# The narrow score tile as one plain fp32 product, five slots for value tiles, and a new order of the streams

## The chip, the cores and the metric

The kernel runs on one core of one Trainium2 chip. The metric is the device time of one execution in microseconds (us); the spans and instruction times below come from one profiled execution. Engines are named as in the profile: PE (TensorE matmul), PEld (its weight loads), ACT (ScalarE), DVE (VectorE), POOL (GpSimd), SP (SyncE, which issues all DMAs here).

## The reference, cut to what matters

Two sequences of 4096 rows with 256 channels pass through single-head causal attention with a residual and a layernorm, then through a router that sends the top 75% of the rows through one 256x256 block with a gelu, then through a residual and a layernorm again.

```python
qkv = x @ w_attn + b_attn
q, k, v = jnp.split(qkv, 3, axis=-1)
attn = jnp.einsum('btc,bsc->bts', q, k) / jnp.sqrt(Cv) + mask      # causal
attn = jax.nn.softmax(attn, axis=-1)
out = jnp.einsum('bts,bsc->btc', attn, v) @ w_proj + b_proj
x = layernorm(x + out)
scores = jnp.einsum('bld,d->bl', x, w_router)                      # top_k: 75% of the rows
processed = gelu(selected @ w_block)
x = layernorm(x + x.at[batch_idx, top_idx].set(processed))
```

All of it is fp32, and which rows are routed hangs on small differences, so the kernel keeps near-fp32 precision in its matmuls.

## The kernel before, in words

**Groups and tiles.** The rows of queries are cut into 16 groups of 512 (8 in each sequence; `G` counts them). The weights of queries and keys are multiplied into one matrix `A` ahead of time, so that the scores of a group are `xT` (the transposed input, the keys' side) against `qT`. A score tile holds 128 keys (partitions) by up to 512 queries (columns). Each group has four tiles on its diagonal, of 512, 384, 256 and 128 columns (tile `i` starts at column `128*i`, `start_col`), and one full tile for each 128 keys before it. The last of the four, 128x128, is the narrow tile of the group. In the last group the diagonal tiles stand at the end of the group, in all others at its start.

**Split products.** Operands of precise matmuls are kept as two fp32r parts, a high one and a low one, made by a rounding copy and a subtraction. `split3` (line 580 on; the matmul itself is line 587) issues three products for each chunk of 128 channels, high by high, high by low and low by high: six matmuls for one score tile.

**Stages of a group.** The projection of queries (`pe_q`) fills a bank of PSUM, ACT writes its high part with a bias (`qhi`, line 932), DVE the low part (`qlo`, line 937). Projected values get the same treatment and go to DRAM (`vstore`, line 985), from where SP loads one 128-row tile at a time into one of `NV` slots of `vs` (`load` in `values`, line 1184): 256 KB each. The load into a slot waits until PE has used its former tile. Scores go to one of two banks `sbank`, ACT copies each into the `ring` of 34 slots (line 1021), DVE adds the mask to diagonal blocks (line 1029) and keeps a running maximum. At the end of a group PE turns the maximum (lines 1111 and 1134), DVE subtracts it (line 1147), ACT takes the exponential (line 1154) and rounds a high part (line 1161), DVE makes the low part (line 1166), and PE multiplies by the values (lines 1230 to 1232 for the first three groups of each sequence, 1236 to 1238 for the others and 1200 to 1202 for the last four tiles). Projection, scores and values of neighbouring groups, and the block behind the router (line 1642 and `split3` into `fbank`), are interleaved on PE.

**What sets the order.** Every piece of work is given to `at(engine, stream, make)`. Within a stream the order is fixed; between the streams of an engine a planner (`planned`) chooses ahead of time, one operation after the other: it holds a table of costs for each engine, takes operations that could start, and prefers the one with the longest chain behind it plus the stream's preference (`PREFER_US`, and `BEFORE_LAST_US` and `LAST_US` in the last two groups); `MARGIN_US` lets a stream's operation be passed over until it has been ready for so long. The result is one fixed list of instructions on each engine, and waits on semaphores between them. The SP list is in order as well: a DMA that must wait holds up those behind it.

**The end.** After the last values PE turns the output back, DVE evaluates the residual and the statistics (`last chain`), a search of eight rounds between DVE and PE (lines 1788, 1844, 1799) finds the threshold of the router, and 16 predicated copies (line 2037) and stores finish. ACT copies the last sums (`ot`, line 1299) and normalizes rows (`norm`, line 1457) there.

Of the kernel before, what the change touches and what calls it, by code (L numbers as in the profile page):

```python
# [16 lines left out]
P = 128  # L17
# [13 lines left out]
NV = 6  # L31
# [28 lines left out]
PREFER_US = {"final result": 2182, "scores copy": 1183, "prepare keys": 1153, "final pick": 1052,  # L60
             "project vhi": 1018, "prepare late": 997, "attention_out aggr": 988, "attention_out norm": 969,
             "project vlo": 917, "prepare xlo": 911, "prepare bias": 864, "project qhi": 759, "project qlo": 745,
             "final load": 741, "attention_out ot": 637, "late load": 622, "final store": 544, "ffn scale": 520,
             "project xlo": 468, "final choose": 418, "search first": 405, "project load": 386, "ffn flo": 367,
             "attention_out store": 363, "ffn rows": 359, "bias columns": 313, "attention_out score": 280,
             "last chain": 188, "row_max": 177, "attention_out load": 128, "attention_out evac": 127,
             "ffn store": 113, "row_max reduce": 93, "softmax lo": 31, "softmax z": 27, "search": 23,
             "softmax hi": -20, "project xhi": -21, "final_roots own": -28, "scores running": -67,
             "attention_out stats": -77, "softmax exp": -128, "attention_out router": -177, "final_roots": -177,
             "ffn fhi": -248, "ffn stats": -290, "ffn gelu": -305, "scores hide": -360, "last": -381,  # L70
             "prepare": -424, "final sums": -456, "last router": -540, "project vstore": -783,
             "attention_out istd": -834, "late": -837, "values load": -896, "attention_out residual": -1389,
             "ffn aggr": -1397, "final own": -1468, "ffn add": -1565, "ffn sums": -1808, "final scale": -1950}
MARGIN_US = {"late": 8, "project xhi": 8, "prepare bias": 8, "final_roots": 8, "attention_out store": 8,
             "final scale": 5, "final sums": 5, "ffn add": 5, "final own": 3, "ffn scale": 3, "prepare keys": 3,
             "ffn rows": 3, "ffn sums": 3, "attention_out norm": 2, "ffn aggr": 2, "ffn stats": 2,
             "final_roots own": 2, "softmax exp": 1.5, "final result": 1.5, "last router": 1.5, "project vlo": 1.5,
             "row_max reduce": 1.5, "search": 1.5, "attention_out residual": 1.5, "project xlo": 1.5,
             "attention_out load": 1.5, "bias columns": 1.5, "late load": 1.5, "values load": 1.5,
             "attention_out score": 1, "attention_out stats": 1, "prepare late": 1, "scores hide": 1,  # L80
             "final load": 1, "project load": 1, "out": 0.6, "proj": 0.6, "attention_out ot": 0.6, "ffn gelu": 0.6,
             "attention_out aggr": 0.6, "ffn flo": 0.6, "final choose": 0.6, "prepare xlo": 0.6,
             "attention_out istd": 0.6, "ffn store": 0.6, "final store": 0.6, "project vstore": 0.6, "scores": 0.3,
             "values": 0.3, "project qhi": 0.3, "project vhi": 0.3, "attention_out evac": 0.3, "search first": 0.3}
BEFORE_LAST_US = {"project xlo": 1066, "attention_out ot": 1012, "final_roots own": 733, "ffn aggr": 721,
                  "project load": 677, "attention_out load": 630, "last router": 576, "prepare keys": 528,
                  "last chain": 492, "final choose": 481, "prepare late": 380, "softmax lo": 322,
                  "row_max reduce": 318, "attention_out residual": 315, "ffn stats": 307, "last": 278,
                  "final sums": 260, "proj": 230, "ffn rows": 224, "project vlo": 141, "project qlo": 134,
                  "search first": 96, "softmax hi": 52, "prepare xlo": 47, "scores copy": 42, "search": 40,  # L90
                  "bias columns": 39, "row_max": 4, "attention_out evac": -7, "attention_out norm": -11,
                  "values": -17, "scores running": -27, "final pick": -39, "ffn flo": -101,
                  "attention_out stats": -105, "attention_out istd": -147, "attention_out aggr": -150,
                  "scores hide": -176, "attention_out store": -188, "project qhi": -193, "out": -211,
                  "ffn gelu": -214, "project vhi": -228, "late": -229, "softmax exp": -229, "softmax z": -245,
                  "values load": -252, "ffn add": -278, "ffn fhi": -300, "ffn sums": -310, "project vstore": -311,
                  "prepare": -321, "late load": -322, "final own": -333, "ffn scale": -374, "prepare bias": -438,
                  "project xhi": -539, "ffn store": -554, "final scale": -560, "final load": -591,
                  "final result": -644, "final_roots": -733, "attention_out score": -873,
                  "attention_out router": -931, "final store": -1016}  # L100
LAST_US = {"last": 970, "final sums": 866, "values load": 854, "project vhi": 796, "ffn scale": 793,
           "final load": 773, "attention_out norm": 684, "attention_out evac": 659, "ffn sums": 657,
           "prepare bias": 651, "search": 552, "softmax hi": 545, "project qlo": 458, "ffn gelu": 411,
           "attention_out residual": 379, "project xlo": 339, "ffn store": 333, "scores hide": 305,
           "project load": 301, "ffn flo": 220, "ffn stats": 218, "ffn fhi": 199, "attention_out store": 146,
           "prepare late": 132, "attention_out ot": 95, "row_max": 90, "final scale": 88, "prepare xlo": 70,
           "softmax lo": 56, "scores running": 48, "attention_out aggr": 30, "scores": 14, "final pick": -5,
           "proj": -17, "late": -63, "attention_out istd": -65, "final_roots": -71, "project qhi": -93,
           "ffn aggr": -117, "search first": -123, "attention_out stats": -131, "last router": -131,
           "row_max reduce": -139, "scores copy": -141, "prepare": -154, "ffn rows": -191, "out": -206,  # L110
# [227 lines left out]
def program(nc, x, xt, w_attn_t, columns, w_proj, b_proj, w_router, w_block, out):  # L338
# [65 lines left out]
    with ctx:  # L404
# [25 lines left out]
        with nc.sbuf_tensor("xraw", [P, CC, GQ], F32) as xraw_:  # L430
            xraw = xraw_
# [1614 lines left out]
        for G in range(len(groups)):  # L2046
            ordered[:] = [G]
            if G:
                project_load(G)
# [127 lines left out]
```

## Time and profile before

| | us |
|---|---|
| median of 3 runs | 954.7 (954.55, 954.7, 959.75) |
| span of the profiled execution | 953.7 |
| PE busy | 931.6 (98%) |
| DVE busy | 785.4 (82%) |
| ACT busy | 633.7 (66%) |
| POOL busy | 305.0 (32%) |
| DMA, mean over 16 engines | 51.0% of the span, 155.84 MB |
| mean granted TensorE clock | 0.992 |

The profiled execution gives its span, 953.7 us from the first instruction to the last; no time of its own outside the span is listed for it, and the median of the runs lies 1.0 us above the span. A PE interval is busy from a matmul's start to its modelled end, so neighbouring matmuls overlap, and the time that a group of them takes is read from its start to the start of what follows.

### The profile page before, as it was taken

Reading aid. Unit: us, or ns where it says so; the run is one execution under the profiler, and the core shown is the slowest. Engines: PE = TensorE matmul, PEld = TensorE weight load, DVE = VectorE, ACT = ScalarE, POOL = GpSimd, SP = SyncE. Lnnn points to the kernel's source line nnn. Section 1 sums busy time; section 2 is a strip of 40 time slices with the busy share of each in tenths; the row PEclk is TensorE's granted clock in tenths of the full one; section 3 lists DMA queues with packets and bytes.
Section 4 is the critical chain, followed back from the end, with each engine's and each line's share of the span. In section 5 each row is a group of like instructions: output and inputs, shape, how many; then the busy total and the mean of one; then the engine's idle time right before and its main releaser. Section 6 shows DMA issues by size and latency. Waiting matters only on the chain.

```text
span 953.7 us, 15684 instructions
## 1 busy us (share of the span) xinstructions
PE 931.6 (98%) x5030; PEld 798.6 (84%) x5030; DVE 785.4 (82%) x1497; ACT 633.7 (66%) x1011; POOL 305.0 (32%) x460
## 2 busy tenths in 40 slices
PE   9999999999999999999999999999999999999992
PEld 6889998888888888888888999888888888888871
DVE  5898887866994896589879999998699799659977
ACT  3576665864774594479565866677578569547994
POOL 3541141242230335333325361452022244301243
PEclk9999999999999999999999999999999999999996
DMA  6644344344353355468634534346777734437934
GB/s 193 206 123 154 104 144 122 103 144 152 101 185 113 111 155 175 146 205 263 195 104 149 189 93 142 130 123 207 234 238 226 242 113 134 150 105 238 323 124 177
DMA packets 89044, 155.84 MB, mean 163 GB/s; under 512 B 8442, under 2 KB 18300, under 8 KB 88964
## 3 DMA queue, kind: packets, MB, share of 16 engines
q1 hardware_dynamic: 88964, 154.85, 51.0%
q8 instruction: 41, 0.67, 0.3%
q14 instruction: 39, 0.32, 0.1%
HBM read 114.96 MB, written 39.86 MB: 162 GB/s over the span
## 4 chain that ended last, share of the span: by engine, by line
PE 85%; DVE 7%; ACT 4%; issue 2%; DMA 1%; DVEq 0%; SPq 0%; ACTq 0%
PE sbank L587 37%; PE fbank L587 12%; PE obank L1236 9%; PE obank L1237 9%; PE obank L1238 9%; PE obank L1232 2%; PE obank L1230 2%; PE obank L1231 2%; DVE ring L1147 1%; ACT parts L1161 1%; DVE ring_lo L1166 1%; ACT ring L1154 1%; DMA ring<-xt 1%; DVE tail L2037 1%; PE mbank L1134 1%
## 5 line engine op out<-in xcount | busy, mean ns | idle before, releaser
L587 PE MATMUL sbank<-qT,xT 128*128 128x512 f32 (+2 forms) x1728 | 406.6, 377 | 1.1 <-ACT ring L1021 1.0
L587 PEld LDWEIGHTS sbank<-qT,xT 128*128 128x128 f32 x1728 | 306.4, 188 | 54.9 <-ACT ring L1021 1.1
L1021 ACT COPY ring<-sbank 128x512 f32<-128x512 f32 (+3 forms) x286 | 157.2, 553 | 178.3 <-PE sbank L587 125.1
L1166 DVE TENSOR_TENSOR ring_lo<-ring,parts 128x1024 fp32r<-128x1024 f32 (+4 forms) x174 | 181.1, 1050 | 32.2 <-ACT parts L1161 31.4
L1161 ACT CAST parts<-ring 128x1024 fp32r<-128x1024 f32 (+4 forms) x174 | 145.0, 843 | 48.1 <-PE obank L1238 34.1
L1070 DVE TENSOR_TENSOR runmax<-ring,runmax 128x1024 f32<-128x1024 f32 x84 | 107.1, 1274 | 69.0 <-ACT ring L1021 68.1
L1147 DVE TENSOR_TENSOR ring<-ring,mbank 128x1024 f32<-128x1024 f32 (+4 forms) x174 | 157.0, 955 | 5.6 <-PE mbank L1134 5.3
L1236 PE MATMUL obank<-ring_lo,vs 128*128 128x512 f32 (+3 forms) x416 | 158.9, 382 | 0.2 <-DVE ring_lo L1166 0.2
L1238 PE MATMUL obank<-parts,vs 128*128 128x512 f32 (+3 forms) x416 | 157.4, 378 | 0.0
L1237 PE MATMUL obank<-parts,vs 128*128 128x512 f32 (+3 forms) x416 | 157.4, 378 | 0.0
L1154 ACT ACTIVATE ring<-ring 128x1024 f32<-128x1024 f32 (+4 forms) x174 | 142.2, 852 | 9.7 <-DVE ring L1147 9.5
L1238 PEld LDWEIGHTS obank<-parts,vs 128*128 128x128 f32 x416 | 78.2, 188 | 14.6
L1236 PEld LDWEIGHTS obank<-ring_lo,vs 128*128 128x128 f32 x416 | 78.3, 188 | 14.3 <-issue 0.9
L1237 PEld LDWEIGHTS obank<-parts,vs 128*128 128x128 f32 x416 | 78.3, 188 | 13.3
L1674 POOL TENSOR_TENSOR yb<-xres,yb 128x512 f32<-128x512 f32 x28 | 39.1, 1418 | 140.2 <-ACT yb L1595 76.5
L1291 POOL TENSOR_TENSOR xres<-xres,b_tot 128x512 f32<-128x512 f32 x30 | 44.5, 1505 | 55.5 <-DMA xres<-x 53.1
L894 POOL TENSOR_TENSOR xT<-xraw,xT 128x512 fp32r<-128x512 f32 x27 | 37.9, 1422 | 64.4 <-ACT xT L876 63.4
L1570 POOL TENSOR_TENSOR ot_sb<-ot_sb,yb 128x512 f32<-128x512 f32 x16 | 22.6, 1413 | 102.5 <-PE fbank L1328 80.1
L587 PE MATMUL fbank<-WV,xT 128*128 128x256 f32 x384 | 51.5, 284 | 0.0
L1065 DVE TENSOR_TENSOR runmax<-ring,runmax 128x512 f32<-128x512 f32 (+3 forms) x73 | 43.3, 594 | 9.7 <-ACT ring L1021 7.6
L587 PEld LDWEIGHTS fbank<-WV,xT 128*128 128x128 f32 x384 | 49.6, 191 | 1.7
L587 PE MATMUL fbank<-xT,A 128*128 128x512 f32 x180 | 46.1, 392 | 0.2 <-DVE qT L937 0.2
(268 smaller groups left out, 1371.4 us busy)
## 6 DMA issues: line engine op xcount, KB each, us to landing
vs<-v_scratch SPq DMA_DIRECT2D x288, 256.0 KB, 2.9
v_scratch<-vnew SPq DMA_DIRECT2D x30, 512.0 KB, 3.5
out<-tail SPq DMA_DIRECT2D x32, 256.0 KB, 2.6
xres<-x SPq DMA_DIRECT2D x15, 512.0 KB, 3.9
x_scratch<-xres SPq DMA_DIRECT2D x14, 512.0 KB, 3.9
y_scratch<-yb SPq DMA_DIRECT2D x14, 512.0 KB, 3.0
tail<-x_scratch SPq DMA_DIRECT2D x28, 256.0 KB, 3.6
tail<-y_scratch SPq DMA_DIRECT2D x28, 256.0 KB, 4.3
```

The source lines that it names most:

```text
L587: mm = eng.matmul(o, lhs(lh, k), rhs(rh, k), start=n == 0, stop=n == len(todo) - 1)
L1021: act.copy(slot(n)[:, c0:], sbank[n % NSS][:, c0:]).then_inc(a_copy, 1)
L1065: dve.tensor_tensor(runmax[:, 0, c0:], slot(n)[:, c0:], runmax[:, 0, c0:], ALU.max).then_inc(v_max, 1)
L1070: dve.tensor_tensor(runmax[:, :, :], slots(ns, 0), runmax[:, :, :], ALU.max).then_inc(v_max, 1)
L1147: dve.tensor_tensor(slots(ns, c0), slots(ns, c0), mbank[:, None, c0:].broadcast_to([P, len(ns), GQ - c0]), ALU.subtract).then_inc(v_z, 1)
L1154: act.activation(slots(ns, c0), slots(ns, c0), ACT.Exp, scale=SCALE).then_inc(a_exp, 1)
L1161: act.copy(hi_of(u), slots(ns, c0)).then_inc(a_hi, 1)
L1166: dve.tensor_tensor(slots_lo(ns, c0), slots(ns, c0), f32(hi_of(u)), ALU.subtract).then_inc(v_lo, 1)
L1236: pe.matmul(o, vh, lo_, start=n == first_tile[G], stop=False)
L1237: pe.matmul(o, vh, hi_, start=False, stop=False)
L1238: mm = pe.matmul(o, vl, hi_, start=False, stop=last)
L1291: pool.tensor_tensor(r[:, 2 * j:2 * j + 2], r[:, 2 * j:2 * j + 2], b_tot[:, None, :].broadcast_to([P, 2, C]), ALU.add).then_inc(g_xres, 1)
```

## The change

The narrow tile is no longer a split product. Two buffers are added, `x_narrow` and `q_narrow`, each 128 partitions by 2 chunks by 128 columns of plain fp32. SP loads `x_narrow` from the transposed input (one DMA for each group, 128 KB), and ACT writes `q_narrow` from the same PSUM bank as `qhi`, with the bias, without rounding to fp32r (two more activations for each group). PE then issues two fp32 matmuls where six fp32r matmuls stood. The low part `qlo` now waits for `q_narrow` as well, ACT waits with `q_narrow` until the narrow tile of the group before has been multiplied, and PE waits with the narrow tile for the load and for `q_narrow`. `NV` falls from 6 to 5. All four preference tables are replaced, which moves instructions on every engine.

```diff
-NV = 6
+NV = 5
...
-PREFER_US = {"final result": 2182, "scores copy": 1183, "prepare keys": 1153, "final pick": 1052,
+PREFER_US = {"final choose": 6932, "prepare keys": 5298, "ffn store": 4854, "scores copy": 4501, "bias columns": 3716,
...
+    narrow_no = {G: n for n, (G, _, i) in enumerate(tiles) if i == QT - 1}
...
+        x_narrow = sb("x_narrow", [P, CC, P])
+        q_narrow = sb("q_narrow", [P, CC, P])
...
+        def narrow_load(G):
+
+            b, g = groups[G]
+
+            def load(sp):
+                if G:
+                    sp.wait_ge(p_s, narrow_no[G - 1] + 1)
+                else:
+                    sp.wait_ge(ld_wv, 16)
+                sp.dma_start(x_narrow[:, :, :], xt_rows[b][:, :, (g + 1) * GQ - P:(g + 1) * GQ]).then_inc(ld_xn, 16)
+            at("sp", "project narrow", load)
...
             act.activation(qT[:, G % 2, 0, m], bank_of(("q", G, m))[:, :], ACT.Identity,
                            bias=ucol[:, m:m + 1]).then_inc(a_qhi, 1)
+                if G:
+                    act.wait_ge(p_s, narrow_no[G - 1] + 1)
+                act.activation(q_narrow[:, m], bank_of(("q", G, m))[:, GQ - P:GQ], ACT.Identity,
+                               bias=ucol[:, m:m + 1]).then_inc(a_qn, 1)
 
             def qlo(dve, m):
                 dve.wait_ge(a_qhi, CC * G + m + 1)
+                dve.wait_ge(a_qn, CC * G + m + 1)
...
-                split3(pe, sbank[n % NSS][:, c0:], lambda h, k: xT[:, h, k, kt * P:(kt + 1) * P],
-                       lambda h, k: qT[:, G % 2, h, k, c0:], CC).then_inc(p_s, 1)
+                if n == narrow_no[G]:
+                    pe.wait_ge(ld_xn, 16 * (G + 1))
+                    pe.wait_ge(a_qn, CC * (G + 1))
+                    for k in range(CC):
+                        mm = pe.matmul(sbank[n % NSS][:, c0:], x_narrow[:, k, :], q_narrow[:, k, :], start=k == 0,
+                                       stop=k == CC - 1)
+                    mm.then_inc(p_s, 1)
+                else:
+                    split3(pe, sbank[n % NSS][:, c0:], lambda h, k: xT[:, h, k, kt * P:(kt + 1) * P],
+                           lambda h, k: qT[:, G % 2, h, k, c0:], CC).then_inc(p_s, 1)
```

**Order on ACT at the start.** Before, `qT` is the high part of the first queries, the copies from `sbank` are those of the first group's four score tiles, and `xT<-ring` is the high part of the next group's input (`xhi`):

```order
L932 ACTIVATE qT<-fbank,ucol 128x512 x2
L876 CAST xT<-ring 128x2x512
L1021 COPY ring<-sbank 128x512
L1021 COPY ring<-sbank 128x384
L876 CAST xT<-ring 128x2x512
L1021 COPY ring<-sbank 128x256
L1021 COPY ring<-sbank 128x128
```

and in the changed kernel (its line numbers are 5 to 33 higher):

```order
L950 ACTIVATE qT<-fbank,ucol 128x512
L954 ACTIVATE q_narrow<-fbank,ucol 128x128
L950 ACTIVATE qT<-fbank,ucol 128x512
L954 ACTIVATE q_narrow<-fbank,ucol 128x128
L1052 COPY ring<-sbank 128x512
L1052 COPY ring<-sbank 128x384
L1052 COPY ring<-sbank 128x256
L894 CAST xT<-ring 128x2x512
```

The two `q_narrow` stand between and behind the two `qT`; the first three score copies now stand ahead of the cast of the next input.

**Order on ACT at the end of the last group**, from the rounding of the 384-column tile (`parts<-ring 128x384`) to that of the last two tiles; `ot_sb` is the copy of the sums, `tail<-xres` the normalization of group 14, `tail<-tail,fin` a final scaling. Before:

```order
L1161 CAST parts<-ring 128x384
L2022 ACTIVATE tail<-tail,fin 128x256 x2
L2027 ACTIVATE tail<-tail,fin 128x256
L1457 ACTIVATE tail<-xres,rstd,rs_h 128x256 x4
L1299 COPY ot_sb<-sbank 128x512 x2
L1161 CAST parts<-xraw 128x256
L1161 CAST parts<-xraw 128x128
```

and now:

```order
L1488 ACTIVATE tail<-xres,rstd,rs_h 128x256
L1192 CAST parts<-ring 128x384
L2058 ACTIVATE tail<-tail,fin 128x256 x3
L2053 ACTIVATE tail<-tail,fin 128x256
L1330 COPY ot_sb<-sbank 128x512 x2
L1192 CAST parts<-xraw 128x256
L2053 ACTIVATE tail<-tail,fin 128x256
L2058 ACTIVATE tail<-tail,fin 128x256
L1192 CAST parts<-xraw 128x128
```

The four normalizations have moved ahead of the rounding of the 384-column tile, so four scalings alone stand directly before the copy of the sums.

**Order on SP at the start**, from the router's weights on. `xres` is the residual input of groups 0 and 1 (512 KB each), `ring<-xt` the transposed input of groups 1 and 2 (512 KB each). Before:

```order
L678 DMA wr<-w_router 128x256
L856 DMA ring<-xt 128x2x512 x2
L1282 DMA xres<-x 128x4x256 x2
L856 DMA xraw<-xt 128x2x512
```

and now:

```order
L683 DMA wr<-w_router 128x256
L1313 DMA xres<-x 128x4x256 x2
L874 DMA x_narrow<-xt 128x2x128
L862 DMA ring<-xt 128x2x512 x2
L862 DMA xraw<-xt 128x2x512
```

The transposed input of the next groups is now issued behind 1 MB of residual input and the new 128 KB.

## Rows read from the trace of the kernel before

**Rows 1.** The page: span, and busy us of each engine (share) and instructions.
```profile
span 953.7 us, 15684 instructions
PE 931.6 (98%) x5030; PEld 798.6 (84%) x5030; DVE 785.4 (82%) x1497; ACT 633.7 (66%) x1011; POOL 305.0 (32%) x460
```

**Rows 2.** Busy time by stretch: start, middle, end; from:to, length, engines, PEclk, DMA, GB/s.
```profile
0.00:30.00 30.00, 27.69 (x147) 21.83 (x148) 15.31 (x42) 11.19 (x17) 13.05 (x40) 1.00 0.62 195
30.00:912.50 882.50, 881.63 (x4746) 761.30 (x4745) 737.23 (x1341) 594.88 (x936) 275.08 (x378) 1.00 0.52 164
912.50:953.70 41.20, 22.24 (x142) 15.44 (x140) 32.85 (x115) 27.65 (x61) 16.86 (x43) 0.81 0.33 122
```

**Rows 3.** Timeline of PE around a narrow tile; start us, us, instruction.
```profile
118.51 0.78 PE L587 MATMUL sbank<-qT,xT 128*128 128x128 f32 x6
119.13 0.33 PE L1230 MATMUL obank<-vs,ring_lo 128*128 128x256 f32 x1
```

**Rows 4.** Groups of PE by line and shape: the narrow tile's matmuls.
```profile
L587 PE MATMUL sbank<-qT,xT 128*128 128x128 f32 x96 | 12.8, 269 | 0.0
```

**Rows 5.** Timeline of PE: plain fp32 matmuls of 256 columns and of one.
```profile
931.88 1.03 PE L1642 MATMUL obank<-runmax,late_x 128*128 128x256 f32 x4
932.75 0.27 PE L1844 MATMUL fbank<-cmp,ones_bf 128*128 128x120 bf16 x2
...
14.10 0.50 PE L704 MATMUL mbank<-bcols,ring 128*128 128x1 f32 x4
14.46 1.31 PE L587 MATMUL sbank<-qT,xT 128*128 128x384 f32 x6
```

**Rows 6.** Groups of ACT by line and shape.
```profile
L1021 ACT COPY ring<-sbank 128x512 f32<-128x512 f32 x240 | 140.2, 587 | 157.4 <-PE sbank L587 106.4 <-PE obank L1238 50.5
L932 ACT ACTIVATE qT<-fbank,ucol 128x512 fp32r<-128x512 f32 x32 | 22.0, 690 | 22.6 <-PE fbank L587 19.4 <-PE fbank L922 3.2
L1021 ACT COPY ring<-sbank 128x128 f32<-128x128 f32 x15 | 3.9, 263 | 3.8 <-PE sbank L587 3.8
```

**Rows 7.** Timeline of the start on PE, ACT and DVE.
```profile
10.41 1.27 ACT L932 ACTIVATE qT<-fbank,ucol 128x512 fp32r<-128x512 f32 x2 [3.23 <-PE fbank L922]
11.13 1.41 DVE L937 SCALAR_TENSOR_TENSOR qT<-fbank,ucol,qT 128x512 fp32r<-128x512 f32 x2 [1.97 <-ACT qT L932]
12.64 1.62 PE L587 MATMUL sbank<-qT,xT 128*128 128x512 f32 x6
15.98 1.04 ACT L876 CAST xT<-ring 128x1024 fp32r<-128x1024 f32 x1 [4.31 <-DMA ring<-xt]
17.57 0.98 PE L587 MATMUL sbank<-qT,xT 128*128 128x256 f32 x6 [1.00 <-ACT ring L1021]
```

**Rows 8.** Busy time by stretch: the last 28 full value tiles, and the DVE's fullest stretch; columns as in rows 2.
```profile
870.70:909.80 39.10, 39.10 (x177) 32.27 (x178) 38.04 (x71) 39.04 (x58) 5.99 (x10) 1.00 0.90 298
...
500.00:600.00 100.00, 100.00 (x648) 90.74 (x647) 94.01 (x225) 68.81 (x116) 43.82 (x65) 1.00 0.44 139
```

**Rows 9.** Value loads: whole program, 870:875, 905:909 (KB each, median us to landing), then their extremes.
```profile
vs<-v_scratch SPq DMA_DIRECT2D x288, 256.0 KB, 2.9
...
vs<-v_scratch SPq DMA_DIRECT2D x2, 256.0 KB, 2.8
...
vs<-v_scratch SPq DMA_DIRECT2D x2, 256.0 KB, 5.6
...
DMA to landing us min/median/max: 2.5/2.9/6.0
```

**Rows 10.** Timeline of SP in the last group: two final loads between value loads.
```profile
900.59 2.91 SPq L1184 DMA_DIRECT2D vs<-v_scratch  x3
903.66 0.32 SPq L1970 DMA_DIRECT2D tail<-x_scratch  x1
904.03 0.42 SPq L1971 DMA_DIRECT2D tail<-y_scratch  x1
904.55 3.02 SPq L1184 DMA_DIRECT2D vs<-v_scratch  x3
```

**Rows 11.** Timeline of the end on PE, ACT and DVE.
```profile
909.55 0.39 PE L1238 MATMUL sbank<-parts,vs 128*128 128x512 f32 x1
...
909.98 2.06 ACT L1457 ACTIVATE tail<-xres,rstd,rs_h 128x256 f32<-128x256 f32 x4
911.95 1.04 ACT L1299 COPY ot_sb<-sbank 128x512 f32<-128x512 f32 x2
...
912.54 0.90 DVE L1312 TENSOR_TENSOR ot_sb<-obank,ot_sb 128x256 f32<-128x256 f32 x2 [2.25 <-ACT ot_sb L1299]
...
912.71 0.28 PE L1202 MATMUL obank<-parts,vs 128*128 128x256 f32 x1
913.11 0.83 PE L1328 MATMUL fbank<-ident,ot_sb 128*128 128x128 f32 x4
...
940.16 9.85 DVE L2037 COPY_PREDICATED tail<-mbank,tail 128x512 f32<-128x512 uint32 x16
```

More of the change, by code:

```diff
@@ L58 @@
 TABLE_US = 1.28
-PREFER_US = {"final result": 2182, "scores copy": 1183, "prepare keys": 1153, "final pick": 1052,
[L61 to L110, printed above, removed]
-           "final store": -206, "project vlo": -231, "final result": -232, "final own": -247, "final choose": -268,
-           "project vstore": -269, "project xhi": -283, "ffn add": -287, "softmax exp": -289, "last chain": -306,
-           "bias columns": -324, "prepare keys": -359, "softmax z": -360, "values": -380, "final_roots own": -398,
-           "attention_out score": -424, "late load": -541, "attention_out router": -610, "attention_out load": -649}
@@ new lines @@
+MARGIN_US = {"late": 14.3, "project load": 11.6, "project vstore": 8, "last": 7, "final choose": 5, "final pick": 5,
+             "final scale": 5, "project xhi": 5, "search first": 5, "bias columns": 4.8, "ffn rows": 4.6,
+             "project narrow": 4, "ffn scale": 3, "final sums": 3, "attention_out istd": 2.6,
+             "attention_out norm": 2.2, "ffn stats": 2.2, "row_max reduce": 2, "final own": 1.8, "final load": 1.7,
+             "ffn flo": 1.5, "ffn gelu": 1.5, "late load": 1.5, "prepare bias": 1.5, "prepare xlo": 1.5,
+             "final result": 1.3, "softmax exp": 1.2, "final_roots": 1.1, "attention_out load": 1, "last router": 1,
+             "project vlo": 1, "project xlo": 1, "attention_out evac": 0.6, "attention_out stats": 0.6,
+             "ffn aggr": 0.6, "final store": 0.6, "out": 0.6, "scores": 0.6, "scores hide": 0.6, "values": 0.6,
+             "attention_out store": 0.5, "values load": 0.5, "attention_out ot": 0.3, "ffn sums": 0.3, "proj": 0.3,
+             "project vhi": 0.3, "search": 0.3, "softmax hi": 0.3, "project qhi": 0.1}
@@ L494, in program @@
         mt_ps = mbank[:, :].rearrange("p (t k) -> p t k", t=QT)
+        ld_xn, a_qn = sem("ld_xn"), sem("a_qn")
         ld_qk, ld_b, ld_w, ld_ffw, ld_xt = sem("ld_qk"), sem("ld_b"), sem("ld_w"), sem("ld_ffw"), sem("ld_xt")
@@ L831, in bias_load @@
                     sp.dma_start(b_cols[:, k:k + 1], b_dram[k * P:(k + 1) * P].rearrange("(p a) -> p a", a=1)).then_inc(ld_bc, 16)
+            narrow_load(0)
             at("sp", "bias columns", bias_store)
@@ L2049, in program @@
                 project_load(G)
+            if G:
+                narrow_load(G)
             project(G)
```

45 lines of the change are left out of this document (added).

## The prediction

> **What bounds the kernel now.** I read the page's busy line first: PE is busy for 98% of a span of 953.7 us, DVE for 82%, ACT for 66% [rows 1]. A mean hides stages, so the busy time by stretch comes next [rows 2]. From 30 us to 912.5 us PE is busy for 881.63 of 882.50 us. In the first 30 us it idles 2.3 us, and in the last 41.2 us it works for little more than half: there DVE and ACT carry the chain. So 92% of the span is the sum of PE's matmuls; what counts there is PE work removed, and any new wait is added in full. The granted clock is 1.00 (2.4 GHz) in the first two stretches, 0.81 on the mean in the end, and nothing in the change gives PE a reason to slow down earlier. The timeline of PE gives prices of work from start to start, which the overlapping durations do not.
>
> **The change part by part**, against the profiled span of 953.7 us; the median of the runs is 1.0 us more.
>
> *The narrow tile on PE.* Six fp32r matmuls start at 118.51 and what follows at 119.13 [rows 3]: 0.62 us, 0.103 us each; there are 96 of them, so 16 tiles [rows 4]. Two plain fp32 matmuls come instead. The trace records a plain fp32 matmul as two weight loads with two matmuls. With 256 columns four such records (two products) take 0.87 us, from 931.88 to 932.75; with one column four take 0.36 us, from 14.10 to 14.46 [rows 5]. 128 columns lie between. The 256-column price is nearer to a price per column, so half of it, 0.43 us, still above the 0.36 us that a record costs without columns; I take 0.43. Gain: 16 x (0.62 - 0.43) = **3.0 us**, all on PE's filled stretch. Bounds: 16 x (0.62 - 0.36) = 4.2 us gained, and 16 x (0.87 - 0.62) = 4.0 us lost.
>
> *`q_narrow` on ACT.* A 128-column copy takes 0.26 us; the bias costs 0.690 - 0.587 = 0.10 us more [rows 6], so 0.37 us, 32 times: 11.8 us of ACT, which has 320 us free [rows 1]. In groups 1 to 15 the queries are projected ahead and other work of PE covers the 0.37 us by which `qlo` is later; without that cover it would be 15 x 0.7 = 10 us at worst. In group 0 nothing covers it: the two `qhi` start at 10.41, `qlo` at 11.13, PE's first scores at 12.64 [rows 7]. With a `q_narrow` behind each `qhi` the second `qlo` starts some 0.7 us later, less the time it stood behind the first: **+0.6 us**.
>
> *The order of the start.* PE waited 1.00 us at 17.57 for a score copy, because ACT stood at the cast of the next input until its DMA landed at 15.98 [rows 7]. Now three copies stand ahead of that cast: -1.0 us. Against it the same input is issued behind 1.1 MB more; at the 195 GB/s of this stretch [rows 2] that is some 5 us, of which PE has two fills of values (24 matmuls) and the narrow tile to work on. I set these against each other, for **-1.0 us** in all, bounds -2 and +3 (the 5 us less some 2 us of moved work).
>
> *The slots of values.* In the last group PE takes 28 tiles in 39.1 us, 1.40 us each [rows 8]. With six slots a load has five tiles, 7.0 us, from its slot being free to its use; with five it has 5.6 us. Loads land after 2.8 us at the beginning of this stretch and 5.6 us at its end; 6.0 us is the longest of the program [rows 9]. Each third one is issued 0.89 us late behind two final loads (903.66 to 904.55) [rows 10]. So in the last third, with the DMA engines at 0.90, a load can be late by 0.9 us; with fewer loads under way each should land a little sooner. A late load stops PE, and the four tiles after it are then early. I take **+0.8 us**; nothing at the low end, and at the high end 28/5 x 0.9 = 5 us. Before that, scores stand between the value tiles, a load has over 10 us, and the cover is wide. Queued behind a held value load are final loads alone.
>
> *The 16 loads of `x_narrow`*: 2 MB on 156 MB, 16 places in SP's list, each held until the narrow tile of the group before is through PE. That tile is at the head of its group and the next one a whole group later (in the last group at its end), so the load has at least 10 us where a value load takes 2.9. **0**, bounds 0 and +1: what is queued behind a held one is a value load, and these have the slack above.
>
> *The end.* PE finished the sums at 909.94. ACT copied them at 911.95 only, since four normalizations stood ahead; DVE waited 2.25 us, and PE could turn the output at 913.11 instead of 912.83 when its own work was through [rows 11]. Now the normalizations come earlier and scalings that need no new data take their place. The copy may be 1 us sooner, of which the first turn takes 0.3 and the second half, whose rounding on ACT and low part on DVE stand behind the same copy, more: **-0.6 us**, bounds -1.5 and +1. The search and the 16 predicated copies (9.85 us) stay as they are.
>
> *The order of the middle.* It has 0.87 us of PE idle to give [rows 2], and small gaps under the modelled ends. What it can lose is open. DVE is at 94% between 500 and 600 us [rows 8], with ACT's new work ahead of it. I take 0, bounds -2 and +5.
>
> Sum: 953.7 - 3.0 + 0.6 - 1.0 + 0.8 - 0.6 = 950.5 us; with the 1.0 us of the runs **951.5 us**.
>
> **The rivals.**
>
> *A: the fifth slot and the new order are paid for by PE (slower).* Place: the last 28 value tiles, and DVE's full stretch. It decides once loads land later than 5.6 us after their slot is free. At 0.9 us in each five tiles that is 5 us instead of 0.8; a further 3 us of waits in the middle gives 951.5 + 4.2 + 3 = 958.7, and the first part alone 955.7. For it: landing times grow to 5.6 us just there. Against it: the median is 2.9 us.
>
> *B: fp32 costs by count of passes (slower).* If a plain product went through PE as four passes at the floor of 0.103 us that the six pay now, the tile would take 8 x 0.103 = 0.83 us: 16 x 0.21 = 3.3 us lost instead of 3.0 gained, 951.5 + 6.3 = 957.8. The trace speaks against the floor being paid four times: it shows two records for each product and 0.09 us for one. The Trainium skill (FP8 and Floating Point Precision, section TensorE Precision Notes) says that true fp32 takes four passes through the array, and so stands against replacing three reduced products by one exact one; by its count the change has eight passes where six were. In streaming time the trace agrees with it: 0.87 us for two products of 256 columns is four clocks of 2.4 GHz for each column.
>
> *C: the new order gives more than I see.* Several small gaps of the middle and of the end go: narrow tile 4.2, start 2, end 1.5, no slot loss, 2 in the middle, about 9 us at most; half of the surplus over my sum gives 947 to 948. Against more: PE's work itself is untouched.
>
> *D: the narrow tile saves nothing* (the new waits on PE, for the load and `q_narrow`, eat it): 951.5 + 3.0 = 954.5.
>
> **How the numbers follow.** My forecast (949 to 953.5) 0.42; D and its neighbourhood (to 955) 0.15; A 0.20, of it 0.04 beyond 1%; B 0.06; C 0.17, of it 0.03 beyond 1%. The range leaves out the outer half of C's reach and the outer parts of A: **946.5 to 958**. A measurement of this kernel tells 1%, 9.5 us, from no change. Faster by more than that (under 945.2) needs all low bounds at once: 0.03. Slower (over 964.2) needs the open loss of the middle beyond its bound: 0.05. Within: 0.92.
>
> **What would show it.** Right: 64 records for the narrow tile, 0.43 us from its start to what follows; PE idle under 2 us between 30 us and the end of the values, and that end near 908 to 909; no PE idle with a value load as releaser; DVE's wait at the sums near 1 us. Wrong: narrow tiles of 0.6 us or more (B, D); PE or its weight loads released by `vs` from 890 us on (A); PE stretches with idle behind DVE in the middle.

## The result: 8 us slower, and the trace after

The changed kernel takes 963.8 us (median of five executions), the kernel before 955.7 us beside it: 1.0082 times the time, 95% interval 1.0064 to 1.0100. One of the five was in a slow state and took 2404.0 us; the ratio leaves it out. The prediction was 951.5 us with a range of 946.5 to 958. It is wrong in sign, and the time lies outside the range.

The profiled execution of the changed kernel has a span of 960.4 us (before 953.7). Its page, which answers to [rows 1]:

```profile
span 960.4 us, 15711 instructions
PE 928.8 (97%) x4998; PEld 793.9 (83%) x4998; DVE 792.4 (83%) x1497; ACT 637.9 (66%) x1041; POOL 310.3 (32%) x460
```

PE works 2.8 us less and idles 31.6 us where it idled 22.1. The windows say where; they are cut, like [rows 2], at 30 us and near the last matmul of the values that PE issues before it first turns the output:

```profile
0.00:30.00 30.00, 27.64 (x148) 21.44 (x149) 16.43 (x43) 12.43 (x22) 12.04 (x40) 1.00 0.65 211
30.00:918.85 888.85, 879.73 (x4712) 757.10 (x4711) 744.19 (x1343) 598.46 (x965) 281.46 (x379) 1.00 0.52 164
918.85:960.40 41.55, 21.42 (x142) 15.36 (x140) 31.74 (x112) 27.06 (x56) 16.82 (x43) 0.80 0.38 138
```

In the first 30 us PE idles as much as before. The middle, which had 0.87 us of PE idle, has 9.12. The cut at the end doesn't fall at quite the same instruction in the two kernels. By the start of the matmul itself (912.71 us before, 918.73 now) the end is 0.7 us longer, and 6.0 of the 6.7 us of span lie ahead of it. PE's granted clock is 1.00 in the first two stretches, as before, and 0.80 in the last (0.81).

The narrow tile on PE, for [rows 3] and [rows 4] (a piece of PE's timeline, then its group):

```profile
119.32 0.61 PE L1033 MATMUL sbank<-q_narrow,x_narrow 128*128 128x128 f32 x4
119.69 0.36 PE L1261 MATMUL obank<-vs,ring_lo 128*128 128x256 f32 x1
119.89 0.28 PE L1262 MATMUL obank<-vs,parts 128*128 128x256 f32 x1
...
L1033 PE MATMUL sbank<-q_narrow,x_narrow 128*128 128x128 f32 x64 | 9.7, 274 | 0.0
```

It is 0.37 us to the next start (before 0.62). But part of the tile is hidden in the spacing of what follows. To the second start behind it there are 0.57 us, and before 0.79:

```profile
118.51 0.78 PE L587 MATMUL sbank<-qT,xT 128*128 128x128 f32 x6
...
119.30 0.28 PE L1231 MATMUL obank<-vs,parts 128*128 128x256 f32 x1
```

So a tile saves 0.22 us and 16 save 3.5. What PE waited for (line and releaser: us, times, longest), the whole span, the longest first:

```profile
PE mbank L1165 <- DVE mcol L1159: 5.1, 5, 1.5
PE mbank L1142 <- DVE runmax L1096: 3.1, 4, 1.5
PE obank L1673 <- issue: 1.9, 1, 1.9
...
PE obank L1267 <- issue: 0.8, 1, 0.8
...
PE obank L1231 <- DMA vs<-v_scratch: 0.3, 1, 0.3
```

The two on top are new: in the kernel before these two waits were 0.2 us each.

```profile
PE mbank L1134 <- DVE mcol L1128: 0.2, 1, 0.2
PE mbank L1111 <- DVE runmax L1065: 0.2, 1, 0.2
```

`L1142` is PE's turning of the running maximum into `mbank` (once for a group, four transposes), `L1165` the turning back of the column of maxima `mcol` that DVE has made of it at `L1152` to `L1159`. PE issues in order. When it comes to one of them and DVE isn't there yet, all the matmuls behind it stand. The fifth slot shows in one wait of 0.3 us. The 0.8 us at `L1267` have no releaser in the view, but their place in time has one, DVE's `ring_lo`:

```profile
702.88 1.20 DVE L1197 TENSOR_TENSOR ring_lo<-ring,parts 128x1024 fp32r<-128x1024 f32 x1
704.18 0.47 PE L1267 MATMUL obank<-ring_lo,vs 128*128 128x512 f32 x1 [0.82 <-issue]
```

### The profile page after: what moved, and what is told of

The parts are those of the page before. It is cut to its first block, busy times and chain, and to the rows that moved or that the text cites. A ratio compares the mean times of both kernels' runs of the same rounds, so it can differ in the third digit from the quotient of the medians.

```text
span 960.4 us, 15711 instructions
## 1 busy us (share of the span) xinstructions
PE 928.8 (97%) x4998; PEld 793.9 (83%) x4998; DVE 792.4 (83%) x1497; ACT 637.9 (66%) x1041; POOL 310.3 (32%) x460
## 4 chain that ended last, share of the span: by engine, by line
PE 79%; DVE 12%; issue 4%; POOL 3%; ACT 1%; DMA 1%; SPq 0%; DVEq 0%; ACTq 0%; POOLq 0%
PE sbank L592 33%; PE fbank L592 11%; PE obank L1269 8%; PE obank L1268 8%; PE obank L1267 8%; DVE ring_lo L1197 2%; DVE ring L1178 2%; PE obank L1261 2%; PE obank L1263 2%; PE obank L1262 2%; DVE runmax L1101 1%; PE mbank L1165 1%; DVE tail L2068 1%; DVE bnst L1385 1%; DVE runmax L1096 1%
## 5 line engine op out<-in xcount | busy, mean ns | idle before, releaser
L592 PE MATMUL sbank<-qT,xT 128*128 128x512 f32 (+2 forms) x1632 | 398.9, 384 | 0.6 <-issue 0.6
L592 PEld LDWEIGHTS sbank<-qT,xT 128*128 128x128 f32 x1632 | 294.4, 188 | 53.4 <-issue 1.0
L1197 DVE TENSOR_TENSOR ring_lo<-ring,parts 128x1024 fp32r<-128x1024 f32 (+4 forms) x174 | 176.7, 1023 | 23.6 <-ACT parts L1192 23.3
L1267 PE MATMUL obank<-ring_lo,vs 128*128 128x512 f32 (+3 forms) x416 | 158.4, 381 | 0.8 <-issue 0.8
L1101 DVE TENSOR_TENSOR runmax<-ring,runmax 128x1024 f32<-128x1024 f32 x84 | 109.3, 1301 | 53.5 <-ACT ring L1052 52.6
L1267 PEld LDWEIGHTS obank<-ring_lo,vs 128*128 128x128 f32 x416 | 78.3, 188 | 15.2 <-issue 1.5
```

Of the source, the lines that this page charges most:

```text
L592: mm = eng.matmul(o, lhs(lh, k), rhs(rh, k), start=n == 0, stop=n == len(todo) - 1)
L1101: dve.tensor_tensor(runmax[:, :, :], slots(ns, 0), runmax[:, :, :], ALU.max).then_inc(v_max, 1)
L1197: dve.tensor_tensor(slots_lo(ns, c0), slots(ns, c0), f32(hi_of(u)), ALU.subtract).then_inc(v_lo, 1)
L1267: pe.matmul(o, vh, lo_, start=n == first_tile[G], stop=False)
```

## Why DVE is late: two kinds of lateness

The longest waits lie at groups 0, 2, 6, 7, 11 and 13. Group 2, on DVE, GpSimd and PE, in the changed kernel:

```profile
75.25 0.69 DVE L1152 TENSOR_REDUCE mcol<-mbank 128x4 f32<-128x512 f32 x1
75.97 0.86 DVE L1157 TENSOR_TENSOR mcol<-mcol,row_const 128x4 f32<-128x4 f32 x1
76.87 1.19 DVE L1159 TENSOR_TENSOR mcol<-mcol,row_const 128x4 f32<-128x4 f32 x1
...
75.51 2.53 POOL L912 TENSOR_TENSOR xT<-xraw,xT 128x512 fp32r<-128x512 f32 x2 [6.47 <-ACT xT L894]
...
78.11 0.65 PE L1165 MATMUL mbank<-ident,mcol 128*128 128x128 f32 x4 [1.35 <-DVE mcol L1159]
```

The same step in the kernel before, with GpSimd idle from 72 to 80 us:

```profile
76.16 0.69 DVE L1121 TENSOR_REDUCE mcol<-mbank 128x4 f32<-128x512 f32 x1
76.88 0.16 DVE L1126 TENSOR_TENSOR mcol<-mcol,row_const 128x4 f32<-128x4 f32 x1
77.08 0.16 DVE L1128 TENSOR_TENSOR mcol<-mcol,row_const 128x4 f32<-128x4 f32 x1
```

Two additions on four numbers per partition, 0.16 us each, take 0.86 and 1.19 us. They end within 0.02 us of the one and the other of GpSimd's two subtractions, which take some 1.3 us each. The reduction ahead of them, which reads PSUM, keeps its 0.69 us. The same happens at groups 0 (0.85 and 1.20 us) and 7 (0.75 and 1.19). So these additions of DVE, with both operands in SBUF, stand still while GpSimd runs its subtraction. The Trainium skill (SBUF — State Buffer, section SBUF: two separate sides) states it: DVE and GpSimd share a pair of ports under an exclusive lock, and a DVE operation with two SBUF inputs waits for the whole of a GpSimd instruction that holds it. The trace agrees with it: both additions end with GpSimd's operations.

The kernel before has such meetings too: one addition takes 1.19 us at group 5, and one 0.53 us at groups 7 and 11. They cost PE 0.2 us in all. At groups 7 and 11 its turning stands 1.1 us and more behind the end of the additions in any case, and at group 5 it waits 0.18 us. What the new order changed is where the meetings fall, and how near PE's row stands behind them.

The second kind is the row. Group 6, DVE and then PE:

```profile
324.64 0.69 DVE L1609 TENSOR_TENSOR x1p<-ot_sb,vnew_b 128x512 fp32r<-128x512 f32 x1 [2.48 <-ACT vnew_b L1605]
326.10 0.29 DVE L1060 TENSOR_TENSOR ring<-ring,mask 128x128 f32<-128x128 f32 x1 [0.77 <-ACT ring L1052]
326.31 0.68 DVE L1152 TENSOR_REDUCE mcol<-mbank 128x4 f32<-128x512 f32 x1
...
327.44 0.65 PE L1165 MATMUL mbank<-ident,mcol 128*128 128x128 f32 x4 [1.55 <-DVE mcol L1159]
```

DVE idles 2.48 us at the head of its row for `x1p`, which waits for ACT and, behind it, GpSimd. It then waits 0.77 us more for the copy that it adds the mask to. The reduction behind both could have started at 323.5. Before, the same two stood ahead of it, but the operand of `x1p` was there at 323.08:

```profile
323.08 1.29 DVE L1578 TENSOR_TENSOR x1p<-ot_sb,vnew_b 128x512 fp32r<-128x512 f32 x2
324.49 0.69 DVE L1121 TENSOR_REDUCE mcol<-mbank 128x4 f32<-128x512 f32 x1
```

## Experiments

The planner sets every row from tables, so any edit moves rows everywhere. To change one thing alone, the runs below take the order of each engine from a list that is written out (`ORDERS`, the rows of one of the two kernels, engine by engine):

```diff
-    orders, times = planned(todo, signalled, urgency(todo), favours)
+    orders, times = pinned(todo)
```

Each time is the median beside runs of the kernel before on the same chip, and the ratio, with its 95% interval, is to those; their median lay between 954.9 and 955.2 us. By the traces e1, e4 and e7 have the changed kernel's sequence of work on PE, ACT, DVE and GpSimd, and e3, e8 and e12 that of the kernel before. **Theory O**: the new order costs it, where PE stands in front of a maximum that DVE has not made. Rivals: **Q** (`q_narrow`'s reads and waits), **S** (the fifth slot), later **P** (GpSimd over DVE), **E** and **W** (a gap closed opens elsewhere).

### Is it the order or the work?

**e1**, the old work in the new order: `before`, ORDERS = rows of the changed kernel without its 16 narrow loads.

> The work of the kernel before (narrow tile as six fp32r products, no q_narrow, no x_narrow, six value slots), but every engine issues its rows in the order of the changed kernel, written out, without the 16 narrow loads. Theory O (the order that the new preferences give makes PE stand in front of turned maxima and maxima columns that DVE has not made yet): the order's cost stays and the narrow tile's saving is gone, so about 4 us above the changed kernel, 966 to 969, with PE idle near 32 us. Rival Q (q_narrow's 32 reads on ACT, and DVE's qlo behind them, cost it): 954 to 957. Rival S (the fifth value slot costs it): 954 to 957, since there are six slots here.

Measured: 962.9 us, ratio 1.0085 (1.0071 to 1.0099). Its waits of PE:

```profile
PE mbank L1200 <- DVE mcol L1194: 4.8, 5, 1.4
PE mbank L1177 <- DVE runmax L1131: 2.8, 3, 1.5
```

The order alone costs 8 us, with none of the new work in the kernel. By the trace nearly all of it lies in the middle: the last matmul of the values starts at 920.52 us, 7.8 us later than before, of 7.9 us of span (961.6). Q and S fall as causes of the order's cost. The figure of 966 to 969 was too high: I had added the whole narrow saving to the changed kernel's time.

**e2**, the new work in the old order: the changed kernel, ORDERS = rows of `before`.

> The work of the changed kernel (fp32 narrow tile from x_narrow and q_narrow, five value slots), but PE, ACT, DVE and POOL issue in the order of the kernel before, written out; the three last tiles of group 8 stand a few rows earlier on PE and ACT, since q_narrow of group 9 waits for them, and SP's loads are moved by up to five rows, with the 16 narrow loads among them. Theory O: the narrow tile's saving of 16 x 0.25 us is left, 955.7 - 4 = 951 to 952.5. Rival Q or S: the cost of 8 us or more comes with the work, 959 to 964.

Measured: 956.3 us, 1.0006 (0.9992 to 1.0021). This is neither case: the 8 us are gone, but the saving isn't there either. One part was my own doing: where the tiles of group 8 had been moved, PE waited 1.3 us at 464.8 for DVE's `row_const`.

**e3**, five slots alone: `before` with

```diff
-NV = 6
+NV = 5
```

> The kernel before with five value slots in place of six and nothing else of the change; its order is written out, SP's loads moved by up to five rows so that none waits for a slot ahead of a store that it holds up. Theory O: 955 to 956.5. Rival S: 960 or more, with PE waiting for vs<-v_scratch in more than one place.

Measured: 955.9 us, 1.0005 (0.9992 to 1.0018); PE waits for a value load once, 0.8 us. S falls: the slot costs about half a microsecond in this order (-0.8 to +1.7 by the interval).

**e4**, `q_narrow` once:

```diff
-                if G:
-                    act.wait_ge(p_s, narrow_no[G - 1] + 1)
-                act.activation(q_narrow[:, m], ...)
+                if G == 0:
+                    act.activation(q_narrow[:, m], ...)
```

> The changed kernel in its own order, but q_narrow is written for group 0 alone and read by all 16 narrow tiles, so that 30 ACT reads of fbank and DVE's waits for them are left out (the narrow tiles of groups 1 to 15 are computed from group 0's queries). Theory O: within 1.5 us of the changed kernel, 962 to 964. Rival Q: back to 955 to 957.

Measured: 963.8 us, 1.0093 (1.0078 to 1.0109). Q falls in this order: DVE waited 11.9 us for `q_narrow` in the changed kernel, and without 30 of the 32 reads nothing is won: the waits at `mbank` are 8.0 us as before (8.2), and the one for `ring_lo` near 705 us has grown from 0.8 to 1.9 us, which may hide a gain of 1 us.

### What in the order?

**e5**, eleven rows moved, on DVE and PE:

```diff
 DVE  + row_max reduce 6   ahead of x1p          PE  + turning back, group 0: 1 row later
      + last maxima 10, 11, 13 ahead of softmax lo    + both turnings, group 2: 1 and 2 rows later
      + row_max reduce 13  ahead of router sums       + turning back, group 7: 2 rows later
```

> The changed kernel with all its work, its order written out and changed in eleven rows alone: on DVE the last steps of the running maximum of groups 10, 11 and 13 stand ahead of softmax lo and of a final result, and the reductions of groups 6 and 13 ahead of x1p and of four router sums; on PE the turning of groups 0, 2 and 7 stands one to three rows later. Theory O (order): the eight gaps of PE in front of mbank, 8.3 us in the trace, go all but a little, so 956 to 957.5. Rival E (the order's cost is spread, and a gap closed here opens elsewhere): 961 or more.

Measured: 960.1 us, 1.0056 (1.0042 to 1.0070). The waits at `mbank` fell from 8.2 to 1.3 us, the time by 3.7 us (medians), the span by 2.6. At 417.8 us PE now waited 1.5 us for `qT` behind a turning that had been moved, and at 420.4 us 1.0 us for `ot_sb`. So a part of the gaps closed came back elsewhere. The time lies between the two expectations.

**e7** moves no row. It lets GpSimd begin later:

```diff
                     pool.wait_ge(a_xhi, G + 1)
+                    if G in (2, 6, 12):
+                        pool.wait_ge(v_mc, 3 * {2: 1, 6: 3, 12: 8}[G])
```

> The changed kernel in its own order; only GpSimd's low halves of xT for groups 2, 6 and 12 wait until the maxima columns of groups 0, 2 and 7 are made. Theory P (while GpSimd's 128x512 subtraction runs, a 128x4 addition of DVE takes 0.75 to 1.2 us in place of 0.16, and PE waits for it): the gaps in front of L1165 at groups 0, 2 and 7 (0.7, 1.4, 1.4 us) go, 960 to 961. Rival: DVE is slow there for another reason, 963 to 964.5.

Measured: 959.6 us, 1.0053 (1.0038 to 1.0068). That is 4.2 us less than the changed kernel by the medians, 4.1 by the spans and 2.8 by the two ratios. DVE and GpSimd at group 2:

```profile
75.60 0.16 DVE L1225 TENSOR_TENSOR mcol<-mcol,row_const 128x4 f32<-128x4 f32 x1
75.80 0.16 DVE L1227 TENSOR_TENSOR mcol<-mcol,row_const 128x4 f32<-128x4 f32 x1
...
76.13 2.54 POOL L980 TENSOR_TENSOR xT<-xraw,xT 128x512 fp32r<-128x512 f32 x2 [7.45 <-DVE mcol L1227]
```

The additions are back at 0.16 us, and PE's waits for `mcol` fell from 5.1 us to 1.7. P holds, and it is some 3 to 4 of the order's 8 us: the low halves, which no one needs for a long time, ran just over the additions on which PE waited.

**e11**, the same wait in e1 (old work, new order).

> The work of the kernel before in the order of the changed one (as the first of these runs, 962.9), with GpSimd's low halves of xT of groups 2, 6 and 12 made after the maxima columns of groups 0, 2 and 7. Theory P: 3.5 to 4.5 us less than without that wait, 958.5 to 959.5, whatever the narrow tile is made of. Rival (the collision comes with the new work): 962 to 964.

Measured: 960.0 us, 1.0052 (1.0039 to 1.0065), against 962.9 for e1: 2.9 us by the medians, 4.7 by the spans (961.6 and 956.9). These collisions come with the order, not with the fp32 tile.

**e9**, e7 and six rows of DVE.

> The changed kernel with GpSimd's wait at groups 2, 6 and 12 as in the run before, and six rows of DVE moved: the reductions of groups 6 and 13 ahead of x1p and of the router sums, the last maxima of groups 11 and 13 ahead of softmax lo and a final result. No row of PE is moved. Theory O+P (what the order costs is PE waiting for mbank, half of it from GpSimd's subtractions over DVE's small additions, half from DVE's row): the gaps left at groups 6, 11 and 13 (1.6, 1.6, 1.4 us) go as well, 955 to 957. Rival E (a gap closed there opens elsewhere): 959 to 960.

Measured: 958.0 us, 1.0032 (1.0021 to 1.0043). 1.6 us of the 4.6: between the two expectations. Around group 13 PE now had two gaps of 1.2 us, one for `ring_lo` (0.6 in e7) and a new one for a score copy. So the next three move one row at a time and leave group 13 alone.

**e13**: e7 and the reduction of group 6 ahead of `x1p` and of the mask. **e14**: and the last maximum of group 11 ahead of a `softmax lo`. **e15**: and on ACT, near the end, the copy into `late_x` ahead of a row that waits for a load (the code moves it past one row, not the two that the expectation names).

> The kernel with GpSimd's wait at groups 2, 6 and 12 (959.6), and one row of DVE moved on top: the reduction of group 6 stands ahead of x1p, which waits for ACT and GpSimd. If a gap of PE in front of mbank is time: the 1.57 us at group 6 go and the end comes 1.2 to 1.6 us sooner, 958.0 to 958.4. If the gap moves on: 959 to 960.

> As the one before, and the last running maximum of group 11 stands ahead of a softmax lo. Its gap of 1.64 us goes, but the turning of the column stands two rows on and DVE is 0.9 us late there (as in e9), so 0.7 us more, 957.3 to 957.7. If nothing is won: as the run before.

> As the one before, and ACT's copy into late_x at the end stands ahead of two rows that wait for a load of y_scratch. If PE's gap in front of L1673 (1.9 us in the changed kernel, told as issue) is that copy: 1.0 to 1.5 us more, 956 to 956.6. If it is PE's own sequencer or a load: as the run before.

Measured: 958.2 us (1.0028, 1.0015 to 1.0040), 957.7 us (1.0025, 1.0012 to 1.0038), 957.1 us (1.0014, 1.0002 to 1.0026). The first is as expected in its median; the other two brought 0.5 and 0.6 us, each within what a pair of runs can tell, and only the way from 1.0053 to 1.0014 is plain. The 957.1 of e15 lie between its two cases. The trace of e13 shows what becomes of a closed gap. Against e7 PE turns the maxima column 1.8 us sooner at group 7 and 1.7 at group 13, but only 0.8 at group 15, and the last matmul of the values starts at the same time (914.42 and 914.46 us). New waits have come in between: 0.6 us for GpSimd's `xT` at 776 us and 0.5 for a value load at 912. So rival E holds in part.

In the changed kernel PE's 1.9 us "issue" in front of `L1673` is ACT at the head of its row:

```profile
927.34 0.51 ACT L2053 ACTIVATE tail<-tail,fin 128x256 f32<-128x256 f32 x1 [0.80 <-DMA tail<-y_scratch]
927.76 0.57 ACT L1651 COPY late_x<-obank 128x512 f32<-128x512 f32 x1
```

PE goes on at 928.42. In e15 that gap is 0.7 us (2.4 in e14's trace), and PE has a wait that was 0.2 us in the changed kernel:

```profile
PE sbank L1707 <- ACT tail L1556: 1.2, 1, 1.2
```

So it was ACT's row, and a good part of its price turned into another wait.

### Where is the saving of the fp32 tile?

**e12**, the tile alone. The kernel before, with all its rows and six slots; the narrow tile reads `wr`, which lies in SBUF anyway, so it leaves out the true scores of that tile:

```diff
+                if n == narrow_no[G]:
+                    pe.wait_ge(ld_ffw, 32)
+                    for k in range(CC):
+                        mm = pe.matmul(sbank[n % NSS][:, c0:], wr[:, k * P:(k + 1) * P], wr[:, k * P:(k + 1) * P], ...)
```

> The kernel before with every row of its order and six value slots; only the narrow tile's six fp32r products are replaced by two fp32 products, of two 128x128 halves of wr with themselves (a tile of the same shape that lies in the chip already), so that no q_narrow, no x_narrow and no slot is needed. It leaves out the narrow tile's true scores. If the fp32 tile is worth what PE's records say (0.62 - 0.37 us, 16 times) and the fifth slot and the reads of q_narrow ate it in the other runs: 950.5 to 951.5. If PE has too little row in reserve and waits take it back by themselves (theory W): 952.5 to 954.5.

Measured: 952.2 us, 0.9972 (0.9960 to 0.9984), span 950.4:

```profile
span 950.4 us, 15636 instructions
PE 928.7 (98%) x4998; PEld 794.5 (84%) x4998; DVE 785.5 (83%) x1497; ACT 633.4 (67%) x1011; POOL 308.8 (32%) x460
```

2.7 us by the runs, between the two expectations, and 3.3 by the spans; the tiles save 16 x 0.22 = 3.5 on PE. PE's idle is 21.7 us (before 22.1), so W, waits that take the saving back by themselves, finds no support in the trace. The median, 0.8 us short of the 3.5, leaves room for a little of it.

**e6**, the new work in the old order without e2's fault; groups 8 and 9, short ones, keep the six products. **e8**, as e2 without that fault, and `q_narrow` only once, as in e4.

> The changed kernel's work in the order of the kernel before, as in the first try of this, but groups 8 and 9 keep the narrow tile of six fp32r products, so that PE and ACT keep every row of the old order there and nothing waits for q_narrow between these short groups; SP's stores of values go ahead of loads that wait. Theory O: 955 - 14 x 0.25 + what the fifth slot costs at the end (about 1) = 951.5 to 953. Rival W (the fp32 tile's own waits give back what it saves on PE, whatever the order): 954.5 to 957.

> The narrow tile in fp32 in the order of the kernel before, five slots, but q_narrow written for group 0 alone and read by all (groups 1 to 15 compute their narrow tile from group 0's queries): the saving on PE without ACT's 30 extra reads and the waits on them. Theory O: 955 - 4 + 1 for the fifth slot = 951 to 952.5, and the difference to the kernel with q_narrow made for each group is what these reads cost, under 1 us. Rival W: 954 or more.

Measured: e6 954.7 us, 0.9997 (0.9988 to 1.0006); e8 953.8 us, 0.9987 (0.9977 to 0.9998). Against e12 (952.2) e8 has the fifth slot, the loads of `x_narrow` and the `q_narrow` of group 0, and takes 1.6 us more. Its waits of PE name the slot and, with no releaser, 0.6 us in front of the first scores:

```profile
PE obank L1333 <- DMA vs<-v_scratch: 0.9, 1, 0.9
PE sbank L658 <- issue: 0.6, 1, 0.6
PE sbank L1333 <- DMA vs<-v_scratch: 0.4, 1, 0.4
```

e6 has the reads of `q_narrow` too, and two fp32 tiles fewer: 0.9 us more, of which the two tiles are 0.4. So by the medians the saving of 2.7 us is given back by what its operands cost: 1.6 us to the slot, the loads of `x_narrow` and the first `q_narrow`, some 0.5 to the other reads, and 0.4 to the two tiles. The interval of each of these runs is about 1 us to either side, so the total is plain and the split is an estimate.

**e10**, e6 with the read of `q_narrow` one row later, behind DVE's low half:

```diff
-                dve.wait_ge(a_qn, CC * G + m + 1)
+            def qnarrow(act, m):
+                act.wait_ge(v_qlo, CC * G + m + 1)
```

> The changed kernel's work in the order of the kernel before, groups 8 and 9 with six fp32r products, and ACT reads q_narrow one row after q's high half, when DVE has made the low half, so that DVE no longer waits for q_narrow. If that wait is what e8 gained over e6: 953.5 to 954. If ACT's own 0.36 us reads are: as e6, 954.5 to 955. If ACT, which now waits for DVE, holds up the copies of scores behind it: over 956.

Measured: 955.4 us, 1.0013 (1.0003 to 1.0022), no better than e6 and between the second and third case. But the edit brought a wait of its own: PE now waits 1.3 us for banks that ACT's later reads still hold.

```profile
PE fbank L662 <- ACT q_narrow L1027: 1.3, 3, 0.6
```

Against that stands a gain at the start, told below. So e10 doesn't tell whether DVE's wait for `q_narrow` was the price.

No version with the true scores beat the kernel before: the nearest, e6, with 14 of the 16 tiles in fp32, is equal to it.

## Why the prediction was wrong

The step that failed is *the order of the middle*: "I take 0, bounds -2 and +5". By e1 the order alone costs 8.1 us (7.8 of it ahead of the end, by the trace), more than its bound by itself. Of it 3 to 4 us are GpSimd's subtractions over DVE's small additions (e7, 2.8 to 4.2 us; e11, 2.9 to 4.7). The rest lies, by the trace, where DVE comes late in its own row. There e13 priced one reduction, 1.4 us by the medians, and e9, e14 and e15 show that of the other gaps only a part comes back; how the rest splits stays open. The last sign of being wrong that the prediction names, PE idle behind DVE in the middle, is the one that came. I had seen that PE has 0.87 us of idle in 882 us and DVE 94% busy between 500 and 600 us, and had called the loss open. That is the sign of a schedule that has no idle left to give, and much to lose: in the trace of the kernel before PE's turning back stands 0.05 to 1.2 us behind the end of DVE's additions in the 16 groups. A bound of 5 us had no row behind it. The rows to read were PE's turnings and what stands ahead of the reduction on DVE in both orders, and how near GpSimd's long operations come to them. Even then the order alone would have misled at group 6, where `x1p` stands ahead in both and only its operand's time differs.

The other steps:
- *The narrow tile on PE*, -3.0 us: right. e12 gives -2.7 (-3.8 to -1.5) and the spans -3.3. With 0.22 us saved of 0.62 a tile costs 0.40 us, midway between the 0.43 that I took and the 0.37 to the next start. Rival B (eight passes at the floor) fell. By the Trainium skill (FP8 and Floating Point Precision, TensorE Precision Notes) true fp32 takes four passes; eight passes of 128 columns at 2.4 GHz are, as an estimate, 0.43 us. The trace agrees with that within 0.03 us: what doesn't hold is the floor of 0.103 us for each pass.
- *`q_narrow` on ACT*, +0.6 us: 0.36 us a read as estimated. PE idles 0.59 us in front of the first scores at 12.82 us, until DVE's second low part ends at 12.72. Every run that reads `q_narrow` right behind `qhi` has this gap (0.59 to 0.60 us). The kernel before, e1, e3, e11 and e12, without `q_narrow`, have none, nor has e10, which reads it later. The other 30 reads cost nothing that shows in the new order (e4) and some 0.5 us in the old one (e6 less e8 less the two tiles).
- *The order of the start*, -1.0 us: the wait of 1.00 us for a score copy is gone, as forecast. A wait of 0.69 us for `mcol` of group 0 has come at 28.55 us, and with it and the 0.59 us above PE idles in the first 30 us as much as before. (The 1.1 MB at 195 GB/s are nearer 6 us than the 5 of the text.)
- *The slots*, +0.8 us: +0.5 in e3, up to 1.6 together with the loads in e8. Right in size. The first half of rival A (load late) fell, its second half (3 us of waits in the middle) is what happened, with two to three times the price.
- *The end*, -0.6 us: +0.7. PE turned the sums 0.28 us sooner behind its last matmul, as forecast, but later ACT stood at the head of its row for a load, and PE waited 1.9 us for the copy into `late_x` (0.4 before). In e1 and e11, where ACT waited for no load, that wait is 0.8 us; in e9 and e14, where ACT waited 1.1 us, it is 2.4.
- *Rival C*: by its own parts, 9 us at most from 954.7, half of the surplus would have been 948.6, not 947 to 948. That changes nothing here.

The sum with measured terms: +8.1 (e1) - 2.7 (e12) + 0.5 (e3) = +5.9, measured +7.8 (955.7 x 0.0082). The 1.9 us left over are within the intervals of these four figures. The trace of the changed kernel has two waits that e1's lacks: 0.6 us in front of the first scores and 1.1 us more in front of `L1673`. Put otherwise, in the new order the new work gains nothing that can be told (1.0082 with it, 1.0085 without); no run takes apart where its saving goes there.

## What to carry over

Where the bound engine is busy without gaps, a new order is not free: give it a price of its own, and read it at the few places where that engine waits in its row for a short chain on another one. Before a long operation of GpSimd is placed, look at which small DVE operations with two SBUF operands it can meet: a wait that delays three pairs of operations, which nobody needed soon, gave back 3 to 4 us. And ask how far behind the bound engine stands: the same meeting costs nothing where it comes a microsecond later. To judge an edit under a planner, write the order out and change one thing; here that took apart the order (+8), the tile (-3) and the slot (about +1), which the changed kernel shows only as a sum. A saving in a product is worth what its operands leave of it.

## What the hardware showed that I had not expected

- An addition of DVE on 128x4 numbers in SBUF takes 0.16 us alone and up to 1.20 us while GpSimd runs a 128x512 subtraction of some 1.3 us; a reduction that reads PSUM keeps its 0.69 us beside it.
- Two plain fp32 products of 128 columns cost PE 0.22 us less than six fp32r products of the same tile (0.57 against 0.79 us to the second start behind).
